# Feed-forward barrier of a decoder layer: VectorE rounds two pieces itself, TensorE multiplies unread data, residual rows get four buffers, the last tile is cut in halves

## The reference, cut to what matters

```python
def quant_per_tensor(x):                       # one scale for the WHOLE tensor
    scale = max(max(abs(x)) / 127, 1e-8)
    return clip(round(x / scale), -127, 127), scale
def dyn_quant_linear(x, w, b):
    qx, sx = quant_per_tensor(x); qw, sw = quant_per_channel(w)
    return (qx @ qw.T) * (sx * sw) + b
h = gelu(dyn_quant_linear(x, w1, b1))          # 3584 x 2048
x = layernorm(x + dyn_quant_linear(h, w2, b2)) # 3584 x 512
```

## Time and profile before

| | |
|---|---|
| median of three runs | 1433.65 us (1432.04, 1433.65, 1437.17) |
| the profiled execution's own time | 1435.72 us |
| its span (first to last instruction) | 1433.9 us |
| busy, share of the span | PE 98%, DVE 75%, ACT 48%, POOL 38% |
| DMA | 149.34 MB, mean 104 GB/s |
| granted PE clock, mean over the span | 0.995 of full |

### The profile page before, as it was taken

How to read it: one execution, slowest core, us unless ns; L and a number is a source line. 1 busy time by engine, 2 the same in 40 slices (tenths; PEclk the granted TensorE clock), 3 DMA queues, 4 the chain that set the end, 5 groups by cost and what they waited for, 6 DMA issues and landing times. The chain is left out here.

```text
span 1433.9 us, 30748 instructions
## 1 busy us (share of the span) xinstructions
PE 1409.3 (98%) x12863; PEld 1119.7 (78%) x12873; DVE 1079.3 (75%) x2010; ACT 685.8 (48%) x995; POOL 543.9 (38%) x499
## 2 busy tenths in 40 slices
PE   9999999999999999999999999999999998999998
PEld 5889898987888888888888888888888885555443
DVE  5888666654568878777787778878768876677898
ACT  2434444442443343443343434434433434888996
POOL 1000000000345444454554444544444542753576
PEclk9999999999999999999999999999999999999999
DMA  7636424232321121121211211211212121438895
GB/s 227 165 100 171 137 96 135 101 113 104 109 73 44 51 80 43 45 72 52 66 57 51 72 37 51 80 46 51 71 45 79 44 63 40 112 134 320 275 347 207
DMA packets 93882, 149.34 MB, mean 104 GB/s; under 512 B 14002, under 2 KB 61746, under 8 KB 91954
## 3 DMA queue, kind: packets, MB, share of 16 engines
q1 hardware_dynamic: 93746, 147.41, 31.4%
HBM read 101.25 MB, written 44.04 MB: 101 GB/s over the span
## 5 line engine op out<-in xcount | busy, mean ns | idle before, releaser
L1177 DVE TENSOR_SCALAR xa_pr<-xa_pr,xa_keep 125x448 f32<-125x448 f32 x384 | 221.3, 634 | 92.9 <-ACT xa_pr L981 92.6
L925 POOL TENSOR_TENSOR xa_psum<-xa_pr 125x448 f32<-125x448 f32 x126 | 166.6, 1322 | 288.0 <-DVE xa_pr L1177 287.1
L981 ACT ACTIVATE xa_pr<-xa_bSC 125x1344 f32<-125x1344 f32 (+2 forms) x192 | 165.8, 916 | 132.4 <-PE xa_bSC L1311 132.4
L961 ACT COPY xa_v<-xa_bKV 125x512 f32<-125x512 f32 x96 | 56.3, 587 | 215.1 <-PE xa_bKV L1240 209.6
L929 POOL TENSOR_TENSOR xa_psum<-xa_psum,xa_pr 125x448 f32<-125x448 f32 x126 | 147.7, 1172 | 10.2 <-PE xa_bPV L1292 0.7
L1229 PE MATMUL xa_bKV<-left_xn,wA 128*128 128x376 f32 x768 | 148.4, 341 | 0.0
L1229 PE MATMUL xa_bKV<-xa_cx,wA 128*128 128x376 f32 x768 | 147.5, 341 | 0.0
L955 ACT ACTIVATE xa_kf<-xa_bKV,xa_bk 128x376 f32<-128x376 f32 x128 | 73.7, 576 | 150.4 <-PE xa_bKV L1229 150.3
L1240 PE MATMUL xa_bKV<-wZ,left_xn 128*125 128x512 f32 x576 | 141.9, 394 | 1.9 <-POOL xa_ones L896 1.9
L1229 PEld LDWEIGHTS xa_bKV<-left_xn,wA 128*128 128x128 f32 x768 | 131.2, 188 | 14.2 <-issue 10.8
L1229 PEld LDWEIGHTS xa_bKV<-xa_cx,wA 128*128 128x128 f32 x768 | 130.2, 188 | 13.7 <-issue 10.0
(11 more groups left out here) (261 smaller groups left out, 2427.1 us busy)
## 6 DMA issues: line engine op xcount, KB each, us to landing
wraw<-in_ctxT SPq DMA_DIRECT2D x32, 752.0 KB, 4.8
ff_hr<-h_scratch SPq DMA_DIRECT2D x28, 512.0 KB, 6.5
wraw<-in_w SPq DMA_DIRECT2D x7, 1024.0 KB, 5.2
xa_qf<-q_scratch SPq DMA_DIRECT2D x32, 224.0 KB, 4.8
xa_x<-x_scratch SPq DMA_DIRECT2D x28, 256.0 KB, 4.8
x_scratch<-xa_x SPq DMA_DIRECT2D x28, 256.0 KB, 2.0
h_scratch<-ff_hq SPq DMA_DIRECT2D x8, 896.0 KB, 4.9
h_scratch<-ff_hs SPq DMA_DIRECT2D x8, 896.0 KB, 5.2
```

The costliest lines, as they stand in the source:

```text
L925: nc.gpsimd.tensor_tensor(psum01[:], third(h, 0), third(h, 1), ALU.add).then_inc(p01_ok, 1)
L981: nc.scalar.activation(pr[h][:, :, t * S:(t + size) * S], bSC[0:TW, :, slot * S:(slot + size) * S], ACT.Exp, scale=XSCALE).then_inc(exp_ok, 1)
L1177: nc.vector.tensor_scalar(third(h, t), third(h, t), EM50, keep[:, b * TC + t:b * TC + t + 1], ALU.max, ALU.min).then_inc(pr_ok, 1)
```

## The change

- Unit 0: the order of PIECES changes (blocks 8 to 11 before 4 to 7). Pieces 0 (one block) and 3 (blocks 8 to 11) are magic-rounded by DVE (`magic_own`), the other four by ACT.
- Unit 1: the upper blocks are narrowed by DVE too, no longer by ACT.
- PE issues six products of weights that lie in SBUF into a bank that nobody reads, before it waits for the spread maximum, and six more after the transpose.
- Residual rows: four buffers `xr`, two in `xt1` as before, two in `hs`. SP issues the rows of units 0 and 1 ahead of the last group's spill, those of unit u + 2 at step u, and the first of these after it has waited for all spills and all maxima. Quarters of `h_scratch` come back from when the first narrow of unit 1 is done. POOL biases three units ahead, not one.
- Last tile: two sets of 16 products of 256 columns, into two banks. DVE evicts, adds and takes statistics for each half, aggregates both, and normalises and sends in three parts.

```diff
-        PIECES = ((0, 1), (1, 2), (2, 4), (4, 8), (8, 12), (12, 16))
+        PIECES = ((0, 1), (1, 2), (2, 4), (8, 12), (4, 8), (12, 16))
+        OWN = (0, 3)
+        NACT = len(PIECES) - len(OWN)
+        XR = 4
+        xr = [xt1[:, UT * p:UT * p + UT, :] for p in range(2)] + [hs[:, p, 0:UT * D].rearrange(...) for p in range(2)]
...
+        SIDES = (slice(0, D // 2), slice(D // 2, D))
+        LAST = ((0, slice(0, D)), (1, SIDES[0]), (1, SIDES[1]))
...
-            eng.wait_ge(hq_ok[0], u + len(PIECES))
-            wait(eng, hq_ok[1], u)
+            eng.wait_ge(hq_ok[0], u + len(PIECES) + 1)
+            wait(eng, hq_ok[1], u - 1)
...
+            def rows(u):
+                sp.dma_start(xr[u % XR], xr_v[u]).then_inc(x2_in[u % XR], 16)
-            groups(sp, spill, RES, NG)
+            groups(sp, spill, RES, NG - 1)
+            sp.wait_ge(xq_ok, 4 * NG)
+            rows(0)
+            rows(1)
+            spill(NG - 1, (NG - 1) % 2)
             for k in range(4):
                 sp.wait_ge(h_out[k], 16 * (NG - RES))
-            sp.wait_ge(xq_ok, 4 * NG)
+            sp.wait_ge(hm_ok, 4 * NG + 2)
...
-                wait(sp, y2_ok, UT * (u - 1))
-                sp.dma_start(xr[u % 2], xr_v[u]).then_inc(x2_in[u % 2], 16)
+                if u + 2 < NU:
+                    wait(sp, y2_ok, UT * (u - 1))
+                    rows(u + 2)
...
-            biased(0)
+            for u in range(3):
+                biased(u)
             for u in range(NU):
+                if u + 3 < NU:
+                    biased(u + 3)
                 if u < NU - 1:
-                    biased(u + 1)
                     norm(u)
...
+            def magic_own(i):
+                h = hidden_part(0, *PIECES[OWN[i]])
+                nc.vector.tensor_scalar(h, h, hx[:, 3:4], ROUND, ALU.mult, ALU.add).then_inc(hown_ok, 1)
...
+                    dve.wait_ge(hsc_ok, 2)
+                    magic_own(0)
...
+                        if i == 1:
+                            magic_own(1)
...
+                if u == 1:
+                    dve.wait_ge(hrnd_ok, NACT + 2 * u)
+                    nc.vector.tensor_scalar(hq[:, u % 2, MA:M, :], hidden_part(u, MA, M), -ROUND, None, ALU.add).then_inc(hq_ok[0], 1)
...
+            def last_side(k):
+                u, cols, bank = NU - 1, SIDES[k], bF[(UT * NU - 1 + k) % 8]
+                i = UT * u + 1
+                dve.wait_ge(q_used, i + 1 + k)
+                nc.vector.tensor_tensor(y[1][:, cols], bank[:, 0:D // 2], s2[:, cols], ALU.mult).then_inc(y_ok, 1)
+                nc.vector.tensor_tensor(acc[u % 3][:, 1, cols], y[1][:, cols], xr[u % XR][:, 1, cols], ALU.add).then_inc(y2_ok, 1)
+                nc.vector.bn_stats(st[:, 1 + k, :], acc[u % 3][:, 1, cols]).then_inc(st_ok, 1)
...
             pe.wait_ge(h_ok, M * NG)
+            idle(6)
             pe.wait_ge(hsp_ok, 1)
             nc.tensor.transpose(bF[1][:, 0:P], spread[:], identf[:]).then_inc(ht_all, 1)
+            idle(6)
...
+                    if u == NU - 1 and j == 1:
+                        pe.wait_ge(y_ok, UT * NU - 7)
+                        for k in range(2):
+                            for m in range(M):
+                                mm = nc.tensor.matmul(bF[(UT * NU - 1 + k) % 8][:, 0:D // 2], hq[:, u % 2, m, P:2 * P], w2q[:, m, SIDES[k]],
+                                                      start=m == 0, stop=m == M - 1)
+                            mm.then_inc(q_used, 1)
```

More of the change, by code:

```diff
@@ L1378, in ffn @@
         xt = [x2_first, xt1[0:S]]
-        xr = [xt1[:, UT * p:UT * p + UT, :] for p in range(2)]
+        XR = 4
+        xr = [xt1[:, UT * p:UT * p + UT, :] for p in range(2)] + [hs[:, p, 0:UT * D].rearrange("p (j d) -> p j d", j=UT) for p in range(2)]
         xqs = n.sb("xqs", [P, GB * D], BF16)
@@ L1507, in _ @@
             results(NU - 2)
-            for j in range(UT):
-                sp.wait_ge(o_last, j + 1)
-                sp.dma_start(out_v[NU - 1][:, j], acc[(NU - 1) % 3][:, j]).then_inc(o_out[(NU - 1) % 3], 16)
+            for i, (j, cols) in enumerate(LAST):
+                sp.wait_ge(o_last, i + 1)
+                sp.dma_start(out_v[NU - 1][:, j, cols], acc[(NU - 1) % 3][:, j, cols]).then_inc(o_out[(NU - 1) % 3], 16)
             for p in range(3):
-                sp.wait_ge(o_out[p], 16 * len(range(p, NU, 3)) + (16 * (UT - 1) if p == (NU - 1) % 3 else 0))
+                sp.wait_ge(o_out[p], 16 * len(range(p, NU, 3)) + (16 * (len(LAST) - 1) if p == (NU - 1) % 3 else 0))
         @block.gpsimd
@@ L1532, in biased @@
             def biased(u):
[L1533 removed]
+                pool.wait_ge(x2_in[u % XR], 16 * (u // XR) + 16)
                 for j in range(UT):
[L1535 removed]
+                    nc.gpsimd.tensor_tensor(xr[u % XR][:, j, :], xr[u % XR][:, j, :], b2t[:], ALU.add).then_inc(x2b_ok, 1)
             def norm(u):
@@ L1601, in _ @@
             act.wait_ge(hsc_ok, 2)
-            for lo, hi in PIECES:
-                h = hidden_part(0, lo, hi)
-                nc.scalar.activation(h, h, ACT.Identity, bias=magic[:, 0:1], scale=hx[:, 3:4]).then_inc(hrnd_ok, 1)
+            for i, (lo, hi) in enumerate(PIECES):
+                if i not in OWN:
+                    h = hidden_part(0, lo, hi)
+                    nc.scalar.activation(h, h, ACT.Identity, bias=magic[:, 0:1], scale=hx[:, 3:4]).then_inc(hrnd_ok, 1)
             for k in range(2):
@@ L1613, in _ @@
                     nc.scalar.activation(h, h, ACT.Identity, bias=magic[:, 0:1], scale=hx[:, 3:4]).then_inc(hrnd_ok, 1)
-                act.wait_ge(hrnd_ok, len(PIECES) + 2 * u)
-                wait(act, q_used, 2 * (u - 2) + 2)
-                nc.scalar.activation(hq[:, u % 2, MA:M, :], hidden_part(u, MA, M), ACT.Identity, bias=minus[:, 0:1]).then_inc(hq_ok[1], 1)
+                if u > 1:
+                    act.wait_ge(hrnd_ok, NACT + 2 * u)
+                    wait(act, q_used, 2 * (u - 2) + 2)
+                    nc.scalar.activation(hq[:, u % 2, MA:M, :], hidden_part(u, MA, M), ACT.Identity, bias=minus[:, 0:1]).then_inc(hq_ok[1], 1)
                 if u >= 3:
@@ L1726, in _ @@
                     narrow(u + 2)
-            for j in range(UT):
-                residual(NU - 1, j)
-                statistics(NU - 1, j, j + 1)
-            for j in range(UT):
+            residual(NU - 1, 0)
+            statistics(NU - 1, 0, 1)
+            last_side(0)
+            last_side(1)
+            statistics_last()
+            for j, cols in LAST:
                 dve.wait_ge(rstd_ok, NU + j)
-                nc.vector.tensor_scalar(acc[(NU - 1) % 3][:, j, :], acc[(NU - 1) % 3][:, j, :], mv[:, j, 0:1], rstd[:, (NU - 1) % 3, j:j + 1],
-                                        ALU.subtract, ALU.mult).then_inc(o_last, 1)
+                nc.vector.tensor_scalar(acc[(NU - 1) % 3][:, j, cols], acc[(NU - 1) % 3][:, j, cols], mv[:, j, 0:1],
+                                        rstd[:, (NU - 1) % 3, j:j + 1], ALU.subtract, ALU.mult).then_inc(o_last, 1)
         @block.tensor
@@ L1811, in _ @@
                 for j in range(UT):
-                    part(u, j, 0, M)
+                    if u == NU - 1 and j == 1:
[5 more added lines that the diff above has]
+                            mm.then_inc(q_used, 1)
+                    else:
+                        part(u, j, 0, M)
 def build(nc, a, out):
```

27 lines of the change are left out of this document (20 added, 7 removed).

## The result

| | before | changed |
|---|---|---|
| median of 14 runs each | 1433.93 us (1432.04 to 1437.17) | 1431.97 us (1429.86 to 1435.64) |
| ratio, with its 95% interval | | 0.9984 (0.9976 to 0.9992) |
| span of the profiled execution | 1433.9 us | 1429.3 us |

The changed kernel is 2.0 us faster. That is less than the 0.3% named as the bound, so the outcome is "within 0.3%". The forecast was 1432.4. Several of its steps were nevertheless wrong, and partly cancelled one another.

A forecast was written before the change was run, and what follows sets the result against it. PE paces layer 2, its end moving only with unit 1's start if DVE and ACT deliver in time, DVE barely. PE's end -0.7 and tail -0.5 give -1.2 us: 1432.4 against 1433.65, range 1429.6 to 1435.4.

The forecast's parts named there:

- The sum: PE's end -0.7 and the tail -0.5 make -1.2 us: 1432.4 against the median of 1433.65; chance 0.50.
- First product: At the barrier, layer 2's first product comes at 1327.5, 0.35 us earlier.
- Unit 0: Layer 2's first unit ends at 1334.7 against 1336.38: 1.7 us earlier, about 1.3 of it clock.
- first rival: At the barrier POOL misses narrow(1); PE gains up to 2.3 us, taking 2.0 the time is 1431.0; chance 0.27.
- The landing of the spills: Early row transfers ahead of the last four spills move the last landing by 0 to 0.5 us, at most 2.8.
- Unit 1: DVE's narrows take turns with POOL's bias pair; unit 1 starts at 1336.65, 0.7 us earlier, bounds 0.7 and 2.3.
- The price of a turn: In unit 1's narrows, DVE and POOL alternate by instruction; one POOL bias instruction takes 1.27 us undisturbed.
- What DVE gives back: In layer 2, narrow(7) ends at 1378.5 where PE wants it at 1378.15: PE loses 0.35 of its 0.7 us.
- second rival: VectorE becomes the bound in layer 2: POOL meets two narrows more, PE ends 2.1 us later, time 1435.3; chance 0.12.
- The sign that I had named for it: In layer 2's profile, PE waiting for DVE's narrow in several units by a microsecond or more.
- The tail: After PE's end, the last tile in halves brings statistics 0.45 us sooner; tail -0.5 us, bounds -0.9 and 0.
- the rival: In the last tile's half products, 16 more weight loads at 98 ns cost 1.6 us, time 1434.0; chance 0.05.

The follow-up runs named there:

- e1: The changed kernel without its twelve unread products at the barrier; ratio to before 0.9988, 107.4 us from second reciprocal to span end.
- e6: The changed kernel again without any edit, second profile; ratio to before 0.9986, 106.9 us from second reciprocal to span end.
- e10: The changed kernel without any edit, third profile; ratio to before 0.9986, 106.5 us from second reciprocal to span end.
- e4: The changed kernel with the scaled product kept in PSUM, not SBUF; ratio to before 0.9988, 105.0 us from second reciprocal to span end.
- e9: The same kernel as e4, run again; ratio to before 0.9977, 105.8 us from second reciprocal to span end.
- e7: The kernel before with only the twelve unread products added; one run, 107.85 us from second reciprocal to span end.
- e11: The kernel before with only the change's residual row handling; ratio to before 0.9999, 107.65 us from second reciprocal to span end.

## Why the prediction was right, and where it was not

**The sum** was right for the median: 1432.4 against 1431.97. It stood on -0.7 at PE's end and -0.5 in the tail. The three profiles of the changed kernel gave +0.15, -0.4 and -0.8 at PE's end, and -0.33 in the tail in the first (the span ends 6.28 us behind PE, 6.61 before), -0.39 and -0.35 in the others. The stretch is shorter by 0.2, 0.8 and 1.2 us, 0.7 in the mean, where the forecast was 1.2. The median fell by 2.0, more than either. That it came so near the forecast value also owes to the reference: 1432.4 was counted from the median of three runs, 1433.65, and that of fourteen is 1433.93. So the number is in part luck.

**First product**: 0.45 us earlier (1.58 to 1.13), forecast 0.35. **Unit 0**: 7.33 us, forecast 7.2 (1327.5 to 1334.7). Without the products unit 1 started 1.1 us later (e1, 9.9 against 8.8); the prediction had 1.0 for this in its first rival, which is the case that came, and called it hidden in the forecast. At PE's end it was hidden again (101.10 against 101.2).

**The landing of the spills: wrong.** I took the share of 0.83 over three microseconds as room for 1 MB, and a delay of 0 to 0.5 us. In a later and longer window of the changed kernel (columns as in rows 2) the queue has no room:

```profile
1318.00:1322.50 4.50, 4.42 (x24) 2.30 (x22) 3.77 (x10) 2.37 (x4) 2.69 (x3) 1.00 1.05 405
```

SP waits 6.2 us for the last spill, where it was 3.5, and POOL's pair comes at 7.92 instead of 5.07: 2.85 later, about what 1 MB takes (2.6 us at 405 GB/s). In two further executions it was 1.5 and 1.6 later. The bound of 2.8 was about right, the value taken was not.

**Unit 1: wrong because of that.** The forecast was 10.4 us after the reciprocal (1336.65 - 1326.26). It came at 8.8 with the pair behind narrow low, which is my first rival, and at 9.7 twice, with the pair in the upper narrow. That second case is the mechanism of the forecast, with one turn rather than two, since the pair came 1.5 us later than before and not 0.5. The price of a turn was about right: 1.88 against 0.96 for 1536 columns. The chain to 1336.65 was also added up too short: it gives the narrows 1.35 and 0.8 us, where its own prices are 1.48 and 0.95; with these unit 1 starts at about 1336.9, 0.4 us earlier than before and not 0.7.

**What DVE gives back: mis-sized.** The prediction worked out a loss of 0.35 us at narrow(7), and then left it out of the sum, which keeps the whole 0.7. The runs showed 2.4, 0.94 and 0.48 of pauses. I reckoned only with the slack at narrow(7), and let PE have at most 0.7 to lose. DVE's pace was in the numbers that I had: 42.65 us for the rounds of units 0 to 5 is 7.1 a round, against PE's 6.92. In the first profile of the changed kernel the same rounds took 42.9 us, from 8.65 to 51.57: DVE's chain began 1.0 us sooner than before, and PE wanted it 2.3 sooner. A chain that is slower than PE up to some unit cannot pass on a gain beyond its slack there, unless its meetings with POOL fall better, as they did in e6 and e10. The slack of 0.35 us was too large as well: before, the first weight load of unit 7 already followed the end of narrow(7) by 0.07 us (52.28 and 52.35 of the stretch), the same distance as at the late units of the changed kernel. The first rival's "taking 2.0" left this out: it expected 1431.0 from unit 1 at 8.8, and the stretch in exactly this case moved by 0.2. My second rival, VectorE as the bound, was right in its mechanism and wrong in its sign: the gain that it cancels came with it. The sign that I had named for it, pauses of a microsecond or more, was too coarse: the longest were 0.65 us.

**The tail**: -0.33 for -0.5. The statistics end 1.83 us behind PE (forecast 1.8), 0.41 sooner than before; the last normalise and the transfers gave nothing back, or cost 0.08. The half products took 0.114 us each (3.66 / 32) where the forecast had 0.109; against 16 whole ones (16 x 0.216 = 3.46) that is 0.2 us more, not the 1.6 of the rival. What the Trainium skill ("TensorE: Matmul & The Clock Gate", section "The mechanism") says of weight loads, that they overlap with a running product only for other rows of the array, is not borne out at 256 columns either. The same section also names loads into a background weight buffer, which the prediction did not take into account.

**What is left open.** The timed runs give some 2.0 to 2.3 us less (0.9984, 0.9986, 0.9986), the stretches 0.7 in the mean. Profiles are single executions and scatter among themselves by 1.0, and ahead of the barrier by several microseconds. Whether the rest lies in executions with better meetings of the two engines, or ahead of the barrier, no run here settles. The same holds for e4 and e9: their stretches are 0.7 to 2.5 shorter than the changed kernel's, and the medians differ by 0.1 us between two sets of runs with the same median of before (1431.86 against 1431.97) and by 1.5 within one set (1431.07 against 1432.54), where the two kernels' intervals overlap. That scarcely any meeting costs time once the product is in PSUM is shown by three profiles only. Why the turns of POOL and DVE fell better in e6 and e10 was not tried either. DVE's share of the barrier work (two magic steps, the upper narrow of unit 1) was never run alone; that it is what moves unit 1 below 11.1 us is inferred from e7 and e11, where the other parts at the barrier left it at 11.1.
